# A graph kernel's dense sum with the nodes split in 834 columns and 15 rows in place of 782 and 16

## What is computed

```python
m = jnp.einsum('ei,ej,ijh->eh', h[dst], edge_attr_8, W_msg_tp) * norm_msg_tp
m = jax.nn.silu(m)
m = m @ W_msg_lin * norm_lin
agg = jax.ops.segment_sum(m, src, num_segments=12500)   # src is in no order
u = jnp.einsum('ni,nh,ihk->nk', h, agg, W_upd_tp) * norm_upd_tp
return x + silu(u) @ W_upd_lin * norm_lin
```

## Time and profile before

| | us |
|---|---|
| median of three runs | 7573.94 |
| lowest and highest run | 7566.49, 7576.72 |
| the profiled execution | 7580.85 |
| its span, first to last instruction | 7579.1 |

### The profile page before, as it was taken

One profiled execution on the slowest core, in us unless ns is written; L12 is line 12 of the kernel. 1 busy time (PEld: TensorE's weight loads), 2 busy tenths in 40 slices (PEclk: granted clock), 3 DMA queues, 4 the chain that ended last, 5 costly groups with the idle time before them and its releaser, 6 DMA issues. The chain is left out here.

```text
span 7579.1 us, 190087 instructions
## 1 busy us (share of the span) xinstructions
PE 6892.4 (91%) x52101; PEld 5979.1 (79%) x52101; DVE 6492.7 (86%) x16891; ACT 4377.7 (58%) x8232; POOL 5712.3 (75%) x4880
## 2 busy tenths in 40 slices
PE   6999999999999999999997699999999999999984
PEld 4777777777777777777776599999999999999981
DVE  6888888888888888888888899999999999999985
ACT  3444444444444444444443577777777777777760
POOL 5777777777777777777776388888888888888880
PEclk9999999999999999999999899999999999999997
DMA  2111111111111111111111454444555555545442
GB/s 53 20 20 20 19 20 20 20 20 20 20 20 20 19 20 20 20 20 20 20 20 33 99 73 73 72 72 71 73 74 71 73 72 72 73 72 74 72 57 39
DMA packets 699525, 333.83 MB, mean 44 GB/s; under 512 B 422354, under 2 KB 643920, under 8 KB 699498
## 3 DMA queue, kind: packets, MB, share of 16 engines
q0 software_dynamic: 336128, 66.50, 15.4%
q1 hardware_dynamic: 362188, 263.59, 13.8%
q10 hardware_dynamic: 1182, 3.44, 0.1%
HBM read 300.69 MB, written 32.35 MB: 44 GB/s over the span
## 5 line engine op out<-in xcount | busy, mean ns | idle before, releaser
L695 POOL DMA_INDIRECT xg<-gather_rows,idx x3232 | 3069.1, 950 | 998.7 <-issue 980.3
L1445 POOL DMA_INDIRECT sums<-total,row x1616 | 2617.9, 1620 | 535.5 <-issue 410.0
L805 PE MATMUL ps_w<-W2s,hT 128*128 128x256 f32 x12928 | 2977.4, 383 | 46.2 <-DVE prod L869 43.4
L805 PEld LDWEIGHTS ps_w<-W2s,hT 128*128 128x128 f32 x12928 | 2431.7, 190 | 562.1 <-DVE prod L869 201.0
L1416 PE MATMUL ps_wide<-hot_col,placed 128*128 128x392 f32 x12928 | 2437.4, 346 | 20.2 <-ACT hot_col L1358 11.4
L1416 PEld LDWEIGHTS ps_wide<-hot_col,placed 128*128 128x128 f32 x12928 | 2317.0, 196 | 51.4 <-issue 39.0
L869 DVE TENSOR_TENSOR prod<-ps_w,xg 128x512 f32<-128x512 f32 x1616 | 1079.6, 689 | 502.3 <-DMA xg<-gather_rows,idx 338.9
L734 ACT ACTIVATE hT<-ps_h,b1c 128x512 f32<-128x512 f32 x1616 | 1018.0, 680 | 312.9 <-PE ps_h L793 312.0
L1257 DVE SCALAR_TENSOR_TENSOR placed<-iota,src_r,halves 128x512 fp32r<-128x512 bf16 x1616 | 1103.1, 744 | 0.1
L1352 ACT ACTIVATE square<-iota_col,minus_col 128x784 bf16<-128x784 int16 x1212 | 1056.4, 934 | 17.0 <-PE ps_wide L1416 17.0
L876 DVE TENSOR_REDUCE msg<-prod 128x32 f32<-128x512 f32 x1616 | 1058.6, 676 | 0.0
(11 more groups left out here) (185 smaller groups left out, 4995.7 us busy)
## 6 DMA issues: line engine op xcount, KB each, us to landing
dst_row<-dst_rows SPq DMA_DIRECT2D x404, 256.0 KB
xg<-gather_rows,idx POOLq DMA_INDIRECT x3232, 2.4
src_row<-src_rows SPq DMA_DIRECT2D x404, 128.0 KB
q_win<-q_rows SPq DMA_DIRECT2D x404, 96.0 KB
ea<-in_edge_attr SPq DMA_DIRECT2D x404, 64.0 KB
sums<-total,row POOLq DMA_INDIRECT x1616, 3.1
e<-in_edge_attr SPq DMA_DIRECT2D x404, 32.0 KB
q_rows<-Q SPq DMA_DIRECT2D x13, 768.0 KB, 3.5
```

Source lines behind the costliest of these rows:

```text
L695: pool.indirect_dma_start(xg[r][:, t, :], None, k.rows, bass.IndirectOffsetOnAxis(ap=idx[r][:, t:t + 1], axis=0)).then_inc(xg_in[r][t], 16)
L805: last = pe.matmul(bank[:, w, :, :].rearrange("p i o -> p (i o)"), hT[half][:, j, col:col + P], k.W2[:, j, :], start=(j == 0), stop=(j == 1))
L1445: pool.indirect_dma_start(k.sums[t], bass.IndirectOffsetOnAxis(ap=row[s][:, t:t + 1], axis=0), total[s][:, t, :], None, compute_op=ALU.add ...
```

## The change

The number of rows goes from 16 to 15, the number of columns from 782 to 834. HM = 15 * 16 / 2 = 120 is half of the rows' features, so the stationary operand is cut in halves of 7.5 rows, 120 columns each; `ps_wide` is filled in 120 partitions. LC becomes 418 and the moving operand has 418 columns. The numbers of matmuls, of loads, of instructions on DVE, ACT and POOL and their order stay as they are; their shapes change: L1257 writes 480 elements instead of 512, L1247 and L1352 836 instead of 784, L1358 2,508 instead of 2,352, L1307 1,672 (four banks of 418) instead of 1,568. As 15 is no power of two, the column of a node comes from a multiplication, a shift by half and a rounding by adding and subtracting 3 * 2^22, three DVE instructions over 1,616 elements a partition once before the loop, in place of a conversion, a shift right and a conversion. The transposes turn 120 partitions, in chunks of 128 columns as before (the last one has 66 in place of 14), and the table is written in runs of 240 elements instead of 256.

```diff
-HR = P // D
-HI = 2 * HR
+HI = 15
+HM = HI * D // 2
+WHOLE = float(3 << 22)
...
-            link(v.tensor_copy(src_i[:, :, :], k.src[:, :, TP:]))
-            link(v.tensor_scalar(src_i[:, :, :], src_i[:, :, :], int(math.log2(HI)), None,
-                                 ALU.arith_shift_right))
-            link(v.tensor_copy(src_col[:, :, :], src_i[:, :, :]))
+            link(v.tensor_scalar(src_col[:, :, :], k.src[:, :, TP:], 1.0 / HI, 0.5 / HI - 0.5,
+                                 ALU.mult, ALU.add))
+            link(v.tensor_scalar_add(src_col[:, :, :], src_col[:, :, :], WHOLE))
+            link(v.tensor_scalar_add(src_col[:, :, :], src_col[:, :, :], -WHOLE))
...
-                v.tensor_tensor(acc[:, :, :], acc[:, :, :], ps_wide[:, :, 0:S.LC],
+                v.tensor_tensor(acc[0:HM, :, :], acc[0:HM, :, :], ps_wide[0:HM, :, 0:S.LC],
                                 ALU.add).then_inc(q["acc_added"], 1)
...
-                                        ps_wide[:, 2 * r + a, 0:S.LC],
-                                        placed[s][:, w, r * HR:(r + 1) * HR, :, part].rearrange("p r f -> p (r f)"),
+                                        ps_wide[0:HM, 2 * r + a, 0:S.LC],
+                                        placed[s][:, w, :, :, part].rearrange("p r f -> p (r f)")
+                                        [:, r * HM:(r + 1) * HM],
                                         hot_col[s][:, w, a, :],
...
-        turned = c_.enter_context(nc.sbuf_tensor("turned", [P, len(chunks), 2, P], f32))
+        turned = c_.enter_context(nc.sbuf_tensor("turned", [P, len(chunks), 2, HM], f32))
...
-                pe.transpose(bank(m)[0:n, :], flat[:, i * P:i * P + n], k.ident[:, :]).then_inc(t_done, 1)
+                pe.transpose(bank(m)[0:n, :], flat[:, i * P:i * P + n], k.ident[0:HM, 0:HM]).then_inc(t_done, 1)
```

More of the change, by code:

```diff
@@ L1112, in layer1 @@
     iota_col = sb("iota_col", [P, 2 * S.LC], i16)
-    src_i = sb("src_int", [P, G, WIDE], i32)
     src_col = sb("src_col", [P, G, WIDE], f32)
@@ L1464, in bank @@
         def bank(i):
-            return ps_wide[:, i % 4, 0:P]
+            return ps_wide[:, i % 4, 0:HM]
         @block.tensor
@@ L1469, in _ @@
             for m, (i, n, r) in enumerate(pieces):
-                flat = acc[:, 2 * r:2 * r + 2, :].rearrange("p a b -> p (a b)")
+                flat = acc[0:HM, 2 * r:2 * r + 2, :].rearrange("p a b -> p (a b)")
                 need(pe, t_copied, m - 3)
-                pe.transpose(bank(m)[0:n, :], flat[:, i * P:i * P + n], k.ident[:, :]).then_inc(t_done, 1)
+                pe.transpose(bank(m)[0:n, :], flat[:, i * P:i * P + n], k.ident[0:HM, 0:HM]).then_inc(t_done, 1)
         @block.scalar
```

## The result

| | before | after |
|---|---|---|
| median | 7570.22 us (4 runs, 7562.07 to 7576.72) | 7647.10 us (4 runs, 7644.53 to 7649.09) |
| the profiled execution | 7580.85 | 7649.09 |
| its span | 7579.1 | 7647.3 |

The change makes the kernel slower by 1.03% (ratio 1.0103, 95% interval 1.0088 to 1.0118). The forecast was 7642 us, +0.9%; the two profiled executions differ by 68.2 us where the sum said 68.5. That agreement is in part luck: two of its terms were off by 8 us each, in opposite directions.

The account below looks back on a forecast made before the run. POOL was taken as the bound at 7.69 us a group, PE second at 7.50; PE's +0.375 makes it the bound. +77.7 us in the loop less 9.2 at its end gives +68.5 on 7573.94: 7642 us, range 7608 to 7680.

Parts of the forecast that it names:

- the sum: Whole kernel: +77.7 us up to group 401's wide sum, 9.2 given back at the end, +68.5 us.
- POOL paces ACT and PE before: Second layer's loop, before: POOL needs 7.69 us a group and delays ACT, then PE, whose own period is 7.50.
- A matmul costs 12.0 ns more: PE's wide sum, L1416: spacing 181 to 193 ns in proportion to moving columns, +0.375 us a group, period 7.875.
- The upper bound of 14.5 ns a matmul: PE's wide sum: conceivable if operand reads come in coarse pieces, +0.46 us a group.
- DVE and ACT cost nothing: Loop: ACT's extra 0.32 us a group is covered by its waits; DVE gets 0.1 us a group shorter.
- POOL begins to wait for rows: POOL's scatters in the loop: they need 7.69 of the new 7.875 us a group, so POOL waits for rows.
- the end takes 34.9 us: End of the loop, from group 401's wide sum to the transposes: 34.9 us instead of 44.06, giving back 9.2.
- Rival A: PE's wide sum: the weight load sets the spacing, PE's period falls to 7.34, total stays 7574 us; chance 14%.
- B: POOL's scatters get shorter, -53 us to 7521 us, if a matmul costs under 181 + 6 ns; chance 5%.
- C: Loop: DVE late by 0.1 us a group holds PE's next gather, 40 us more, 7682 us; chance 8%.
- the signs that I had named: Profile after: L1416 up 12 ns, 32 spanning 6.40 us, ACT's landing waits under 400 us, POOL gaps not all 0.30.

Follow-up runs that it names:

- e5_before_3sc: Kernel before the change, with POOL scattering only three of a group's four tiles: 7493.6 us, ratio 0.9898.
- e4_move256: Changed kernel with PE streaming only 256 of 418 moving columns: 8780.6 us, one run where the kernel before took 8781 or 8818 us.
- e1b_move392: Changed kernel with PE streaming only 392 of 418 moving columns, on another chip: 7566.8 us against 7565.0 for the kernel before, ratio 0.9995.
- e8_after_colfirst: Changed kernel with DVE's L1247 moved ahead of its four L1257, same work and result: 7637.7 us.
- e7_after_odd: Changed kernel with DVE's L1247 split into two instructions of 417 and 419 columns, same result: 7646.6 us.

## Why the prediction was right, and where it was not

- **POOL paces ACT and PE before, PE has 0.18 us to spare.** Shown by e5_before_3sc: 7.681 to 7.500. e4_move256, at 7.660 with 2.3 us less on PE, agrees.
- **A matmul costs 12.0 ns more.** Measured 11.4. The 26 moving columns alone cost the 12.0 that proportionality gave; the 8 stationary ones give back 0.6, which the sum had at nothing inside a block. With the exposed first load PE's period rose by 0.350 us instead of 0.375: 7.464 to 7.850 for the columns, +0.386, and 0.036 back for the 8 stationary ones, which the sum had at 0.007. This is the mis-sized term: 400 x 0.025 = 10 us too many, less 2 us in which the change's loop is longer than PE's own period (7.854 against 7.850 in the three changed kernels where ACT hardly waits for landings), 8.1 in all at group 401 (7418.77 against 7426.85). The Trainium skill's gap of N / 2.4 + 2.5 ns ("TensorE: Matmul & The Clock Gate", section "Back-to-back issue gap") would have given 10.8 ns, 0.6 too few where the sum had 0.6 too many, and 0.347 us a group, though its 166 and 177 ns stand against 181 and 192. The upper bound of 14.5 ns a matmul had no row behind it, and no run came near it.
- **DVE and ACT cost nothing.** Shown by e1b_move392 for the two together (DVE's `placed` got shorter as ACT's tiles grew), and by ACT's waits, which remain.
- **POOL begins to wait for rows, and the end takes 34.9 us.** Wrong. I took 4 x 1.921 for POOL's need and 7.69 < 7.875 for a surplus. But its shortest period is 4 x 1.855 = 7.42, and the rest is for the most part waiting for DVE inside the scatter, which no wait shows and which isn't fixed. At 7.85 the scatters were held longer, by 0.15 us a group, POOL stayed as far behind as before, and the end took 43.04 us: 8.1 us more than the sum. That this met the 8.1 us of the loop was chance. With L1247 moved or split on DVE, ACT's waits for landings go, and the end takes 37.4 us (e8_after_colfirst) or 39.8 (e7_after_odd). (4 x 1.921 is 7.68, not 7.69, and the bounds add up to 7610 to 7682; neither slip matters.)
- **Rival A** (the load sets the spacing) fell with 32 x 418 at 190 ns. **B** (shorter scatters, faster) fell: they got longer, and the matmul's price was above its condition of 6 ns. **C** (DVE late) fell: DVE waits for PE now.
- Of the signs that I had named, L1416's 346 + 12 came as 357, 32 in 6.40 us as 6.38, and PE's idle time went to nothing; ACT's wait fell to 422, not below 400, and POOL's gaps stayed at 0.30.

The median's rise, 76.9 us, is more than the 68.2 of the profiled executions, because the profiled execution of before was at the upper end of its runs.

## What to carry to other kernels

Moving columns are paid one by one (26 of them 0.386 us a group here), stationary columns are nearly free while the load hides (8 of them 0.036): cut the count of moving columns, and fill the 128 stationary ones. When one engine has a slack of 0.18 us a period, a change of 0.35 on it shows as the difference; take the engine's own period from where the other bound isn't active (the first groups of the loop, here). And the busy time of a transfer-issuing engine isn't its need. Its mean holds waits for another engine, which move with that engine; its shortest instruction gives a floor alone (4 x 1.855 = 7.42 us here, where POOL still held the loop at 7.68 and not at PE's 7.50). Whether it paces the loop is told by a run with one transfer fewer.

## What the runs showed of the hardware that was not expected

- fp32r matmuls at 2.4 GHz take 13.9 to 17.7 ns over the pure stream, for 256 to 418 moving columns, at a slope of 0.44 to 0.46 ns a column; at 1.2 GHz the same matmul takes 314 to 338 ns, around its stream of 327.
- A scatter that runs into DVE's L1257 (two tensor inputs) is held as one that runs into L1247 (one input) is, until 0.10 or 0.12 us after DVE's end in the kernel before, 0.17 or 0.09 in the changed one. Odd column counts didn't change that. They made DVE slower only as two instructions in place of one: 391 columns took 0.47 us on average and 393 took 0.41, where 784 in one instruction take 0.65.
- With four scatters a group their mean followed the loop: 1.62 us at a period of 7.68, 1.66 at 7.85, 1.67 at 7.89. POOL looked fully occupied in all three. With three a group it was 1.66 at 7.50 and 1.70 at 7.85, with POOL idle for a third of the time.
